# T masked before the weight split, no GpSimd copy, and hinted branches at the head of a LoRA feed-forward kernel

## The chip, the cores and the metric

The kernel runs on 1 core of one Trainium2 chip. The metric is device time in microseconds (us) of one execution. Three runs of the kernel before took 905.58, 907.25 and 908.7 us, the median is 907.25 us.

## The reference

Input `x` has 128 sequences of 32 tokens with 512 features, all float32; `itok_B_2_6` gives each sequence one of 16 LoRA adapters (values 2 to 6 are drawn). With B[i], A[i] chosen by a sequence's adapter:

```
lora_add(base, inp, A, B) = base + 0.5 * (inp @ A[i].T) @ B[i].T        # rank 16
gate = lora_add(x @ W_gate.T, x, A_gate, B_gate)                        # 512 -> 1376
up   = lora_add(x @ W_up.T,   x, A_up,   B_up)
act  = silu(gate) * up
down = lora_add(act @ W_down.T, act, A_down, B_down)                    # 1376 -> 512
amax = clip(max(|down|, axis=-1), 1e-5)
out  = x + (down / amax) @ levels[weight_2bit].T * (amax * weight_scale) + bias
```

## The kernel before

The host sorts nothing. The kernel itself ranks the 128 sequences by adapter (the "plan": `make_plan` on VectorE and one TensorE product, L1945), so that a tile of 512 tokens (16 sequences) holds at most two adapters. A flag `plan_flag` says whether this is so; each of the five engines reads it (`pair_flag`, L399) and branches to `wide_program` (8 tiles of 512 tokens, which is what runs on these inputs) or `general_program` (16 tiles of 256 tokens). On SyncE and TensorE the wide part is the `Else` of the branch (L730, L1954) and lies behind the whole general part in the program; on the other three engines it is the `If`.

Float32 products are made of three products of split numbers: ScalarE copies the high part of an operand (`_hi`), VectorE subtracts it from the whole for the low part (`_lo`), and TensorE multiplies high by high, low by high and high by low (`PASSES`). The 1376 inner features are 11 chunks, the first 96 wide and ten 128 wide. The 32 unused columns of the first chunk's weights hold the LoRA A matrices of the tile's two adapters, so that the first chunk's products (`first_tile_chunks` for tile 0, L1781) also give t = A x in 32 partitions of the banks `pw_gate` and `pw_up`. VectorE multiplies this t with a mask of 0.5 and 0 that keeps each token's own adapter (`wide_mask_t`, L1370). The masked t is written three times into `wt_split`: its high part in rows 0 to 31 (ScalarE, `wide_t_hi`, L1006), its low part in rows 32 to 63 (VectorE, `wide_t_lo`, L1375), and its high part again in rows 64 to 95 (semaphore `t_hi_again`). The B matrices are laid out to match in `wb_split` (ScalarE L999 for 64 rows, VectorE L1347 for 32), so that one product of 96 rows (`wide_lora`, L1813) adds the LoRA term. TensorE waits for `t_lo`, `t_hi_again` and `b_lo` before the first of these, and for `wgu_lo` (weights of chunk f split) and `silu_done` before the products of chunk f from 2 on (L1771).

The order of work is written out by hand for each engine. In tile 0 weights still come in: ScalarE and SyncE ask for gate and up weights (`load_wgu`, 512 KB each) and down weights (`load_wd`), two staging places each, and an ask for chunk f waits for the split of chunk f - 2. In tile 0 the second copy of the high part is made by GpSimd (L823); in the others by ScalarE. In tile 0, x comes in 16 entries of 64 KB (one sequence each, from a place that is read out of the plan, `load_x_entry`, L329): entries 0 to 7 (`x_raw`) by SyncE and ScalarE in turn before the branch, entries 8 to 15 (`x_more`) after it, three by ScalarE (`FROM_POOL` is 3) and five by GpSimd. SyncE's wide program begins with the mask, the two adapter numbers and the B rows (`load_wide_b`, L370).

TensorE runs 13 and 17 warm-up products ahead of its branch and 7 after it (`warm_up`, L1762), and then the products of tile 0, first for the first 256 tokens, then for the second.

Of the kernel before, what the change touches and what calls it, by code (L numbers as in the profile page):

```python
# [10 lines left out]
ALU = mybir.AluOpType  # L11
# [17 lines left out]
PAIR = 2 * RANK  # L29
# [14 lines left out]
WIDE = 512  # L44
# [24 lines left out]
FROM_POOL = 3  # L69
# [13 lines left out]
def build(nc, x_tok, x_feat, lora_index, places, pair_masks, w_gu, w_down, w_2bit, a_gu, a_down, b_rows,  # L83
          scale_col, bias_rows,
          block_mask_in, identity_in, out):
    with ExitStack() as ctx:
# [380 lines left out]
        def _(sp):  # L467
# [157 lines left out]
            def wide_program():  # L625
                load_mask(sp, 0, mask_gu, mask_gu_in)
# [97 lines left out]

            sp.dma_start(idx_places, lora_index).then_inc(index_in, 16)
# [4 lines left out]
            with sp.If(flag == 0):  # L730
                general_program()
            with sp.Else():
                wide_program()

        @block.gpsimd
        def _(pool):
# [81 lines left out]
            def wide_program():  # L818
                for e in range(FROM_POOL, ENTRIES):
                    load_x_entry(pool, wide_place(0, ENTRIES + e), x_more[:, e, :], pool_x_in)  # L820
                for g in range(2):
                    pool.wait_ge(t_masked, g + 1)
                    pool.tensor_tensor(wt_split[2 * PAIR:STACK, g, :], t_full[:, g, :],  # L823
                                       ones[0:PAIR, :].to_broadcast([PAIR, WIDE]), ALU.mult).then_inc(t_hi_again, 1)
                wide_split_bd(0, first=True)
                wide_split_a(1)
                pool.wait_ge(const_in, 48)
                with pool.Fori(1, WTILES - 1) as tile:
                    wide_split_a(tile + 1)
                    wide_split_bd(tile)  # L830
                    for s in range(WSUBS):
                        bias_residual(tile - 1, s)
                pool.wait_ge(residual_biased, WSUBS * (WTILES - 2))
                wide_split_bd(WTILES - 1)
                for s in range(WSUBS):
                    bias_residual(WTILES - 2, s)
                pool.wait_ge(late_res_in, 16 * WENTRIES)
                for s in range(WSUBS):
                    late = x_late[s // 2][:, s % 2, :]
                    pool.tensor_tensor(late, late, bias[:, :], ALU.add).then_inc(residual_biased, 1)  # L840
# [14 lines left out]
        def _(act):  # L855
# [146 lines left out]
            def wide_t_hi(tile, g, first):  # L1002
                act.wait_ge(t_masked, 2 * tile + g + 1)

                for first_row, done in (((0, t_hi),) if first else ((0, t_hi), (2 * PAIR, t_hi_again))):
                    nc.scalar.activation(wt_split[first_row:first_row + PAIR, g, :], t_full[:, g, :], ACT.Copy  # L1006
                                         ).then_inc(done, 1)
# [45 lines left out]
            def wide_tile(tile, first):  # L1053
# [7 lines left out]
                if first:  # L1061
                    for e in range(1, FROM_POOL):
                        load_x_entry(act, wide_place(0, ENTRIES + e), x_more[:, e, :], x_more_in)
                    load_wgu(act, 2)
                wide_x_hi(tile, 1, first)
                if first:
# [5 lines left out]
                    wide_t_hi(tile, 0, first)  # L1072
                    wide_t_hi(tile, 1, first)
                    split_hi_wd(0)
                else:
# [3 lines left out]
                    wide_t_hi(tile, 0, first)  # L1079
                    wide_t_hi(tile, 1, first)  # L1080
# [72 lines left out]
        def _(dve):  # L1153
# [277 lines left out]
            def wide_tile(tile, first):  # L1431
# [8 lines left out]
                if first:  # L1440
                    split_lo_wgu(2)
                    wide_b_lo(tile, 0)
                    wide_b_lo(tile, 1)
                    wide_mask_t(tile, 0, pw_gate, first)
                    wide_mask_t(tile, 1, pw_up, first)
                    wide_t_lo(tile, 0)
                    wide_t_lo(tile, 1)
                    split_lo_wd(0)
# [143 lines left out]
        def _(pe):  # L1592
# [350 lines left out]

            pe.wait_ge(plan_steps, PLAN_COLUMNS_STEP)
# [9 lines left out]
            with pe.If(flag == 0):  # L1954
                general_program()
            with pe.Else():
                wide_program()

# [63 lines left out]
```

## Time and profile before

| | us |
|---|---|
| median of three runs | 907.25 |
| lowest, highest | 905.58, 908.7 |
| profiled execution | 907.95 |
| its span | 906.1 |
| TensorE busy in it | 890.4 |
| VectorE, ScalarE, GpSimd busy | 350.9, 259.2, 87.2 |

The span runs from the first to the last instruction of one profiled execution, the time around it is 1.85 us. PE is TensorE, DVE VectorE, ACT ScalarE, POOL GpSimd, SP SyncE; a q behind a name is the sequencer of the engine, which reads registers, branches and issues DMAs. A time in the rows counts from the start of the span. "Idle before" is how long an engine did nothing ahead of a group, with what ended it.

### The profile page before, as it was taken

To read this page: it belongs to the slowest core of one execution; us is meant where nothing else is said; L and a number is where in the kernel's file an instruction comes from. 1 tells how busy PE (TensorE), PEld (TensorE's weight loads), DVE (VectorE), ACT (ScalarE), POOL (GpSimd) and SP (SyncE) were. 2 spreads that over 40 slices of the span, in tenths; PEclk is the share of its full clock that TensorE was granted. 3 is DMA by queue.
4 is the path that set the end of the run, shared out by engine and by line. 5 is a ranking of instruction groups with operands and counts; after the bars stand their busy time and mean duration, and the time that the engine had idled before them with its cause. 6 is when DMAs were issued, how large, how long until landed. Compare 5 with 4: busy or idle time off the path is not lost.

```text
span 906.1 us, 13800 instructions
## 1 busy us (share of the span) xinstructions
PE 890.4 (98%) x3991; PEld 720.2 (79%) x3991; DVE 350.9 (39%) x757; ACT 259.2 (29%) x448; POOL 87.2 (10%) x119
## 2 busy tenths in 40 slices
PE   6899999999999999999999999999999999999997
PEld 6788888888888887888888888788878888788885
DVE  4755264233442225422453224432245322552225
ACT  2533252122422124211242113421143111522112
POOL 1111003000030000310003100031001210100200
PEclk9999999999999999999999999999999999999999
DMA  5563110211112011120111102111111111201001
GB/s 144 166 192 109 39 56 22 51 30 33 47 35 59 21 45 45 31 62 12 50 48 38 47 12 57 52 38 35 27 45 52 43 33 30 56 24 34 24 14 47
DMA packets 44661, 45.38 MB, mean 50 GB/s; under 512 B 13168, under 2 KB 31088, under 8 KB 44608
## 3 DMA queue, kind: packets, MB, share of 16 engines
q1 hardware_dynamic: 42208, 41.52, 16.9%
q10 hardware_dynamic: 2176, 2.89, 1.1%
q0 software_dynamic: 224, 0.46, 0.2%
q14 instruction: 43, 0.35, 0.1%
q8 instruction: 10, 0.16, 0.1%
HBM read 36.44 MB, written 8.39 MB: 49 GB/s over the span
## 4 chain that ended last, share of the span: by engine, by line
PE 95%; DVE 1%; DMA 1%; ACT 0%; issue 0%; SPq 0%; ACTq 0%; DVEq 0%
PE pw_up L1771 26%; PE pw_gate L1771 24%; PE pw_down L1844 24%; PE ps_misc L1872 6%; PE pw_td L1833 5%; PE pw_down L1857 2%; PE pw_up L1813 2%; PE ps_misc L1771 2%; PE pw_gate L1813 2%; PE ps_misc L1864 1%; DMA rows<-w_gu 1%; DMA x_raw<-x_feat 0%; DVE wt_split L1375 0%; DMA plan_room<-places 0%; PE ps_misc L1813 0%
## 5 line engine op out<-in xcount | busy, mean ns | idle before, releaser
L1844 PE MATMUL pw_down<-wd,wact_split 128*128 128x512 f32 x960 | 232.5, 391 | 0.0
L1771 PE MATMUL pw_up<-wxs,wgu 128*128 128x512 f32 x948 | 229.4, 391 | 0.0
L1844 PEld LDWEIGHTS pw_down<-wd,wact_split 128*128 128x128 f32 x960 | 180.3, 188 | 44.5
L1771 PE MATMUL pw_gate<-wxs,wgu 128*128 128x512 f32 x864 | 212.8, 395 | 0.1
L1771 PEld LDWEIGHTS pw_up<-wxs,wgu 128*128 128x128 f32 x948 | 178.4, 188 | 38.6
L1771 PEld LDWEIGHTS pw_gate<-wxs,wgu 128*128 128x128 f32 x864 | 161.2, 189 | 33.6 <-issue 0.5
L1395 DVE TENSOR_TENSOR wact_full<-pw_up,wact_full 128x512 f32<-128x512 f32 (+1 forms) x87 | 60.0, 690 | 297.2 <-PE pw_up L1813 294.9
L1025 ACT ACTIVATE wact_full<-pw_gate 128x512 f32<-128x512 f32 (+1 forms) x80 | 47.7, 597 | 279.3 <-PE pw_gate L1813 279.3
L1037 ACT ACTIVATE wact_split<-wact_full 128x512 fp32r<-128x512 f32 x80 | 50.5, 631 | 69.7 <-DVE wact_full L1395 69.7
L1400 DVE TENSOR_TENSOR wact_split<-wact_full,wact_split 128x512 fp32r<-128x512 f32 x80 | 55.7, 697 | 26.3 <-ACT wact_split L1037 26.3
L815 POOL TENSOR_TENSOR rows<-rows,bias 128x512 f32<-128x512 f32 x28 | 35.8, 1288 | 222.3 <-DMA rows<-x_tok 221.1
L1872 PE MATMUL ps_misc<-wq,wdt_split 128*128 128x512 f32 x224 | 55.3, 389 | 0.0
L792 POOL TENSOR_TENSOR wgu_first<-wa_raw,scales 128x64 fp32r<-128x64 f32 x28 | 8.3, 327 | 446.8 <-DMA wa_raw<-a_gu 446.8
L1833 PE MATMUL pw_td<-wact_split,wad_split 128*32 128x512 f32 (+1 forms) x160 | 50.4, 397 | 0.0
L1872 PEld LDWEIGHTS ps_misc<-wq,wdt_split 128*128 128x128 f32 x224 | 42.0, 188 | 8.7
L1428 DVE SCALAR_TENSOR_TENSOR rows<-ps_misc,scales,rows 128x512 f32<-128x512 f32 x28 | 21.0, 751 | 71.8 <-PE ps_misc L1872 57.5
L999 ACT ACTIVATE wb_split<-low_room 64x256 fp32r<-64x256 f32 x40 | 16.8, 420 | 97.2 <-PE pw_up L1813 97.2
L1813 PE MATMUL pw_up<-wt_split,wb_split 96*128 96x512 f32 (+1 forms) x87 | 34.1, 392 | 0.0
L1813 PE MATMUL pw_gate<-wt_split,wb_split 96*128 96x512 f32 (+1 forms) x80 | 31.7, 396 | 2.3 <-DVE wt_split L1375 2.3
L1421 DVE TENSOR_TENSOR wdt_split<-ps_misc,wdt_split 128x512 fp32r<-128x512 f32 x28 | 19.3, 689 | 37.5 <-ACT wdt_split L1050 37.5
L999 ACT ACTIVATE wb_split<-wb_raw 64x256 fp32r<-64x256 f32 (+1 forms) x48 | 18.6, 403 | 47.8 <-PE pw_up L1813 47.2
L1006 ACT ACTIVATE wt_split<-wact_full 32x512 fp32r<-32x512 f32 x30 | 18.9, 630 | 41.0 <-DVE wact_full L1370 40.4
(137 smaller groups left out, 678.2 us busy)
## 6 DMA issues: line engine op xcount, KB each, us to landing
out<-rows SPq DMA_DIRECT2D x121, 64.0 KB, 1.6
rows<-x_tok SPq DMA_DIRECT2D x112, 64.0 KB, 1.8
rows<-w_gu SPq DMA_DIRECT2D x8, 512.0 KB, 3.9
x_raw<-x_feat SPq DMA_DIRECT2D x60, 64.0 KB, 1.7
x_more<-x_feat SPq DMA_DIRECT2D x56, 64.0 KB, 1.8
wb_raw<-b_rows SPq DMA_DIRECT2D x32, 92.0 KB, 2.9
low_room<-b_rows SPq DMA_DIRECT2D x32, 80.0 KB, 2.5
rows<-w_down SPq DMA_DIRECT2D x9, 256.0 KB, 4.1
```

The source lines that it names most:

```text
L815: pool.tensor_tensor(wx_res[:, s % 2, :], wx_res[:, s % 2, :], bias[:, :], ALU.add).then_inc(residual_biased, 1)
L999: nc.scalar.activation(wb_split[0:2 * PAIR, f % 2, :, 0:WIDTHS[f]], wb_raw_chunk(f), ACT.Copy).then_inc(b_hi, 1)
L1025: nc.scalar.activation(wact_full[0:w, f % 2, :], gate_bank(f)[0:w, :], ACT.Silu).then_inc(silu_done, 1)
L1037: nc.scalar.activation(wact(HI, f), wact_full[0:WIDTHS[f], f % 2, :], ACT.Copy).then_inc(act_hi, 1)
L1395: nc.vector.tensor_tensor(wact_full[0:w, f % 2, :], up_bank(f, first)[0:w, :], wact_full[0:w, f % 2, :], ALU.mult).then_inc(act_done, 1)
L1400: nc.vector.tensor_tensor(wact(LO, f), wact_full[0:WIDTHS[f], f % 2, :], wact(HI, f).bitcast(F32), ALU.subtract).then_inc(act_lo, 1)
L1428: nc.vector.scalar_tensor_tensor(wout[:, s, :], bank, ascale[:, s:s + 1], residual, ALU.mult, ALU.add).then_inc(out_ready, 1)
L1771: last = nc.tensor.matmul(bank, w, wxs[:, xp, k, :], start=(n == 0 and k == 0), stop=False, skip_group_check=(f == 0))
L1813: nc.tensor.matmul(bank[0:w, :], wb_split[0:STACK, f % 2, g, 0:w], wt_split[0:STACK, g, :], start=False, stop=True, skip_group_check=(f == ...
L1833: last = nc.tensor.matmul(pw_td[0:m, :], wad_split[0:w, f % 2, 0:m], wact(part, f), start=(f == 0 and part == HI), stop=(f == FC - 1 and p ...
L1844: last = nc.tensor.matmul(pw_down[:, s, :], wact(ap, f)[:, s * P:(s + 1) * P], wd[:, wp, f, :], start=(f == 1 and n == 0), stop=False)
L1872: last = nc.tensor.matmul(bank, dt[:, part, k, :], wq[:, k, :], start=(part == HI and k == 0), stop=(part == LO and k == KC - 1))
```

## The change

VectorE masks t ahead of the B splits and of the weight split of chunk 2. GpSimd no longer copies the high part in tile 0; ScalarE makes both copies of both halves, first copies first, in all tiles. `FROM_POOL` goes from 3 to 5: GpSimd asks for x entries 13 to 15, ScalarE for 8 and 9, SyncE for 10 to 12, as the first thing of its wide program. On SyncE and TensorE a branch-hint instruction stands at the head of the program, and the branch to the wide part is marked likely.

```diff
--- before.py
+++ after.py
@@ -66,7 +66,8 @@
 LAST_BY_ACT = [range(0), range(2, 4), range(1, 4), range(2, 4)]
 
 
-FROM_POOL = 3
+FROM_SP = 2
+FROM_POOL = 5
 PLAN_COLUMNS_STEP = 8
 WQ_FROM = FC - KC
 
@@ -623,6 +624,8 @@
                                  .rearrange("a t n -> (a t) n")).then_inc(done, 16)
 
             def wide_program():
+                for e in range(FROM_SP, FROM_POOL):
+                    load_x_entry(sp, wide_place(0, ENTRIES + e), x_more[:, e, :], x_more_in)
                 load_mask(sp, 0, mask_gu, mask_gu_in)
                 idx = wide_loras(0)
                 load_wide_b(sp, idx, 0)
@@ -722,15 +725,21 @@
                     store_wide_at(sp, last, s, entries, places[s])
                 sp.wait_ge(stored, 16 * WENTRIES * WTILES)
 
+
+            to_wide = sp.mark_branch_hint_location()
             sp.dma_start(idx_places, lora_index).then_inc(index_in, 16)
             sp.wait_ge(plan_listed, 1)
             for e in range(0, ENTRIES, 2):
                 load_x_entry(sp, wide_place(0, e), x_raw[:, e, :], x_in)
             flag = pair_flag(sp)
-            with sp.If(flag == 0):
+            sp.br_cond(flag == 1, on_true="sp_wide", on_false="sp_general").branch_hint(to_wide)
+            with nc.body("sp_general", valid_engines=[mybir.EngineType.SP]):
                 general_program()
-            with sp.Else():
+                sp.br("sp_end")
+            with nc.body("sp_wide", valid_engines=[mybir.EngineType.SP]):
                 wide_program()
+                sp.br("sp_end")
+            nc.switch_bb("sp_end")
 
         @block.gpsimd
         def _(pool):
@@ -818,10 +827,6 @@
             def wide_program():
                 for e in range(FROM_POOL, ENTRIES):
                     load_x_entry(pool, wide_place(0, ENTRIES + e), x_more[:, e, :], pool_x_in)
-                for g in range(2):
-                    pool.wait_ge(t_masked, g + 1)
-                    pool.tensor_tensor(wt_split[2 * PAIR:STACK, g, :], t_full[:, g, :],
-                                       ones[0:PAIR, :].to_broadcast([PAIR, WIDE]), ALU.mult).then_inc(t_hi_again, 1)
                 wide_split_bd(0, first=True)
                 wide_split_a(1)
                 pool.wait_ge(const_in, 48)
@@ -999,12 +1004,13 @@
                 nc.scalar.activation(wb_split[0:2 * PAIR, f % 2, :, 0:WIDTHS[f]], wb_raw_chunk(f), ACT.Copy
                                      ).then_inc(b_hi, 1)
 
-            def wide_t_hi(tile, g, first):
-                act.wait_ge(t_masked, 2 * tile + g + 1)
-
-                for first_row, done in (((0, t_hi),) if first else ((0, t_hi), (2 * PAIR, t_hi_again))):
-                    nc.scalar.activation(wt_split[first_row:first_row + PAIR, g, :], t_full[:, g, :], ACT.Copy
-                                         ).then_inc(done, 1)
+            def wide_t_hi(tile):
+                for first_row, done in ((0, t_hi), (2 * PAIR, t_hi_again)):
+                    for g in range(2):
+                        if done is t_hi:
+                            act.wait_ge(t_masked, 2 * tile + g + 1)
+                        nc.scalar.activation(wt_split[first_row:first_row + PAIR, g, :], t_full[:, g, :], ACT.Copy
+                                             ).then_inc(done, 1)
 
             def wide_td_copy(tile):
                 act.wait_ge(td_done, FC * (tile + 1))
@@ -1059,7 +1065,7 @@
                     load_x_entry(act, wide_place(0, ENTRIES), x_more[:, 0, :], x_more_in)
                 wide_x_hi(tile, 0, first)
                 if first:
-                    for e in range(1, FROM_POOL):
+                    for e in range(1, FROM_SP):
                         load_x_entry(act, wide_place(0, ENTRIES + e), x_more[:, e, :], x_more_in)
                     load_wgu(act, 2)
                 wide_x_hi(tile, 1, first)
@@ -1069,15 +1075,13 @@
                     load_wd(act, 1)
                     wide_b_hi(tile, 0, first)
                     wide_b_hi(tile, 1, first)
-                    wide_t_hi(tile, 0, first)
-                    wide_t_hi(tile, 1, first)
+                    wide_t_hi(tile)
                     split_hi_wd(0)
                 else:
                     wide_act_hi(tile - 1, FC - 1, False)
                     wide_b_hi(tile, 0, first)
                     wide_b_hi(tile, 1, first)
-                    wide_t_hi(tile, 0, first)
-                    wide_t_hi(tile, 1, first)
+                    wide_t_hi(tile)
                     wide_td_copy(tile - 1)
                     wide_td_hi(tile - 1)
                 for f in range(FC):
@@ -1438,13 +1442,13 @@
                 wide_x_lo(tile, 0)
                 wide_x_lo(tile, 1)
                 if first:
-                    split_lo_wgu(2)
+                    wide_mask_t(tile, 0, pw_gate, first)
+                    wide_mask_t(tile, 1, pw_up, first)
                     wide_b_lo(tile, 0)
                     wide_b_lo(tile, 1)
-                    wide_mask_t(tile, 0, pw_gate, first)
-                    wide_mask_t(tile, 1, pw_up, first)
                     wide_t_lo(tile, 0)
                     wide_t_lo(tile, 1)
+                    split_lo_wgu(2)
                     split_lo_wd(0)
                 else:
                     wide_act_lo(tile - 1, FC - 1)
@@ -1941,6 +1945,8 @@
                 wide_ffn(last, 2, last_bank[2], last_dt(2))
                 wide_ffn(last, 3, last_bank[3], last_dt(3))
 
+
+            to_wide = pe.mark_branch_hint_location()
             pe.wait_ge(plan_steps, PLAN_COLUMNS_STEP)
             nc.tensor.matmul(ps_plan, plan_columns, one_hot, start=True, stop=True).then_inc(plan_gathered, 1)
             pe.wait_ge(wgu_hi, 2)
@@ -1951,10 +1957,14 @@
                 nc.tensor.matmul(pw_td[:, :], wgu_chunk(HI, 1)[:, 0, 0, :], wgu_chunk(HI, 1)[:, 0:2, :, :],
                                  start=True, stop=True)
             flag = pair_flag(pe)
-            with pe.If(flag == 0):
+            pe.br_cond(flag == 1, on_true="pe_wide", on_false="pe_general").branch_hint(to_wide)
+            with nc.body("pe_general", valid_engines=[mybir.EngineType.PE]):
                 general_program()
-            with pe.Else():
+                pe.br("pe_end")
+            with nc.body("pe_wide", valid_engines=[mybir.EngineType.PE]):
                 wide_program()
+                pe.br("pe_end")
+            nc.switch_bb("pe_end")
 
 
 def kernel(x, itok_B_2_6, L0_cond_W_gate, L0_cond_W_up, L0_cond_W_down, L0_cond_A_gate, L0_cond_B_gate,
```

## Rows read from the trace of the kernel before

**Rows 1.** Part 1 of the page: busy us, share of span, instructions.

```profile
PE 890.4 (98%) x3991; PEld 720.2 (79%) x3991; DVE 350.9 (39%) x757; ACT 259.2 (29%) x448; POOL 87.2 (10%) x119
```

**Rows 2.** Timeline, TensorE, 0 to 50 us: start, duration, group, [idle before].

```profile
15.05 1.10 PE L1762 MATMUL ps_misc<-wgu 128*128 128x256 f32 x7 [0.39 <-issue]
15.98 0.64 PE L1781 MATMUL pw_gate<-wxs,wgu_first 128*128 128x256 f32 x4
...
26.06 1.60 PE L1781 MATMUL pw_down<-wxs,wgu 128*128 128x256 f32 x12
29.96 0.47 PE L1813 MATMUL pw_gate<-wt_split,wb_split 96*96 96x512 f32 x1 [2.29 <-DVE wt_split L1375]
...
31.21 4.51 PE L1771 MATMUL pw_gate<-wxs,wgu 128*128 128x512 f32 x12
...
42.47 2.88 PE L1771 MATMUL pw_gate<-wxs,wgu 128*128 128x512 f32 x12
```

**Rows 3.** Busy time by window: window, length, engines, granted clock, DMA share, GB/s.

```profile
31.20:35.72 4.52, 4.51 (x13) 3.62 (x14) 4.21 (x8) 4.05 (x8) 0.00 (x0) 0.64 0.80 191
```

**Rows 4.** Timeline, all engines, 24 to 30 us.

```profile
24.13 1.23 DVE L1156 TENSOR_TENSOR wgu<-rows,wgu 128x1024 fp32r<-128x1024 f32 x1 [1.87 <-ACT wgu L858]
24.14 0.64 PE L1781 MATMUL pw_up<-wxs,wgu_first 128*128 128x256 f32 x4
...
24.52 0.67 ACT L999 ACTIVATE wb_split<-wb_raw 64x192 fp32r<-64x192 f32 x2 [0.42 <-DMA wb_raw<-b_rows]
...
26.10 0.69 DVE L1370 TENSOR_TENSOR wact_full<-pw_gate,low_room 32x512 f32<-32x512 f32 x1
...
26.83 1.24 ACT L1006 ACTIVATE wt_split<-wact_full 32x512 fp32r<-32x512 f32 x2 [1.64 <-DVE wact_full L1370]
26.88 2.48 POOL L823 TENSOR_TENSOR wt_split<-wact_full,scales 32x512 fp32r<-32x512 f32 x2 [9.65 <-DVE wact_full L1370]
27.49 2.41 DVE L1375 TENSOR_TENSOR wt_split<-wact_full,wt_split 32x512 fp32r<-32x512 f32 x2
```

**Rows 5.** Line L1375 over the whole run: ns min/median/max, first and last start.

```profile
L1375 DVE TENSOR_TENSOR wt_split<-wact_full,wt_split x16: 681/683/1516, 27.5 to 782.0; 32x512 fp32r<-32x512 f32 x16
```

**Rows 6.** Lines L730, L381, L384 and L1954, columns as in rows 5.

```profile
L730 SPq COMPARE_BRANCH  x1: 50/50/50, 12.2 to 12.2; - x1
...
L381 SPq TENSOR_LOAD <-plan x16: 263/268/460, 14.7 to 879.5; - x16
...
L384 SPq MOVE low_room<-pair_masks x1: 29/29/29, 15.4 to 15.4; - x1
L384 SPq DMA_DIRECT2D low_room<-pair_masks x1: 354/354/354, 16.8 to 16.8; - x1
...
L1954 PEldq COMPARE_BRANCH  x1: 3659/3659/3659, 11.3 to 11.3; - x1
```

**Rows 7.** Timeline, SyncE's queue, 0 to 50 us.

```profile
7.91 3.70 SPq L329 DMA_DIRECT2D x_raw<-x_feat  x4
...
18.69 1.75 SPq L370 DMA_DIRECT2D wb_raw<-b_rows  x4
```

**Rows 8.** Chain; DMA issues of page and 0 to 40 us; queues 12 to 14 us; ScalarE.

```profile
11.27 3.42 DMA x_raw<-x_feat
...
x_raw<-x_feat SPq DMA_DIRECT2D x60, 64.0 KB, 1.7
...
x_more<-x_feat ACTq DMA_DIRECT2D x3, 64.0 KB, 2.9
...
q8 instruction: 1, 0.02, 3.4%
...
19.95 1.06 ACT L990 ACTIVATE wxs<-x_more 128x1024 fp32r<-128x1024 f32 x1 [4.17 <-DMA x_more<-x_feat]
```

**Rows 9.** Timeline, ScalarE, 37 to 47 us.

```profile
38.41 0.63 ACT L863 ACTIVATE wd<-rows 128x512 fp32r<-128x512 f32 x1 [2.54 <-DMA rows<-w_down]
...
39.90 0.58 ACT L1025 ACTIVATE wact_full<-pw_gate 128x512 f32<-128x512 f32 x1
```

## The prediction

> **What bounds the kernel now.** Read first the busy shares of the page: TensorE is busy 890.4 us of a span of 906.1 us [rows 1], so only what delays it can move the time, and nearly all its idle time is at the two ends. Then read TensorE in the timeline of the first 45 us [rows 2]. The reader is to see three places: 0.39 us idle ahead of the second warm-up, 2.29 us idle at 29.96 us ahead of the first tile's LoRA products, and twelve products from 31.21 us that take 4.51 us where the same twelve take 2.88 us at 42.47 us. The windows [rows 3] explain the third: in 31.20 to 35.72 us the mean granted clock is 0.64, a mix of full speed (2.4 GHz) and half (1.2 GHz), right behind the 2.29 us in which TensorE did nothing. So one hole costs twice: 2.29 us, and 4.51 - 2.88 = 1.6 us of slow products. The other engines in front of the hole [rows 4] show what made it. The two LoRA-A results are complete at 24.14 + 0.64 = 24.78 us, but VectorE masks them only from 26.10 us, after the weight split (1.23 us) and the two B splits. Then GpSimd copies (2.48 us for two) while VectorE subtracts, and VectorE's two subtractions take 2.41 us; over the whole run one takes 0.68 us in the median and 1.52 us at most [rows 5].
>
> **The change part by part.**
>
> *Mask first.* The mask products need their bank (first one about 24.3 us, second 24.78 us) and the mask, which SyncE asked for at 16.8 us. VectorE is idle then, so two masks of about 0.69 us end at 25.05 and about 25.7 us, against 27.4 us now. The mask is no longer what ScalarE waits for: it is the B rows. ScalarE starts on them at 24.52 us, waiting for their landing [rows 4], and its two B splits take 0.67 us, so it is free at 25.2 us.
>
> *No GpSimd copy, two more ScalarE copies.* ScalarE now makes four copies in a row. Two take 1.24 us, so four take 2.5 us: 25.2 to 27.7 us. VectorE's subtractions follow the second copy (26.4 us) and take 0.68 us each without GpSimd beside them: done at 27.15 us. So the fourth copy ends last, at 27.7 us, and it takes the place of the subtraction that ended at 29.90 us. TensorE's preceding products end at 26.06 + 1.60 = 27.66 us [rows 2], so it starts the LoRA products at about 27.75 us: the hole shrinks from 2.29 us to 0.1 us, 2.2 us gained. Removed from GpSimd are 2.48 us which nobody else waits for.
>
> *Weight split 2 moved behind.* It runs 27.15 to 28.4 us on VectorE. ScalarE's first down-weight split and first silu (0.63 and 0.58 us for one of each in [rows 9]) end at about 28.8 us, so the products of chunk 2 start at 28.85 us against 31.21 us: 2.35 us gained in all at this point. The split is not free (1.23 us) but lies beside the silu.
>
> *Clock.* With 0.1 us idle, then four LoRA products, then some 0.2 us idle, I take no fall of the granted clock: 1.6 us gained. From the other side it is 0, if the rest of the hole is enough for a fall; I take 1.6 because the only fall in these rows follows 2.29 us without any product.
>
> *What is late next.* TensorE's chunk 3 starts at 42.47 us [rows 2]; it needs silu 2, which ends at 39.90 + 0.58 = 40.48 us, held by a down-weight landing at 38.4 us [rows 9]. That is a cover of 2.0 us. This supply chain hangs on VectorE's order (down-weight split, ask, land), and VectorE comes to its first down-weight split at 28.4 us instead of 29.90 us (27.49 + 2.41): 1.5 to 1.6 us earlier. TensorE moves 2.35 + 1.6 = 3.95 us. 2.0 + 1.6 - 3.95 = -0.35 us: a wait of about 0.35 us appears there. For later chunks I take none.
>
> *SyncE's three x entries.* Each is a load of a register, a few register steps and a DMA: four take SyncE 3.70 us from the first DMA's start to the last one's end, and a DMA some 0.35 us [rows 6, 7], so it is 1.1 us from one to the next. Three put 3.3 us ahead of the mask and the B rows. One is taken from ScalarE, two from GpSimd, which did them without a stop. They are hidden as long as the split of the second half of x starts by about 20.6 us; it starts at 19.95 us now [rows 8], takes 1.06 us, and TensorE begins the second half midway between 15.98 us and the end of the last group's issue, 27.5 us, at 21.7 us.
>
> *SyncE's hint.* SyncE's branch is recorded at 12.2 us with 0.05 us, and its next instruction starts at 14.7 us [rows 6]: 2.4 us in which nothing is issued. Five instructions later it stands again: the register step at 15.4 us, the DMA it belongs to at 16.8 us, 1.3 us, where a whole x entry takes 1.1 us. If the hint removes the first stop, the second still can stand, since the code behind the target is asked for only after the jump. With the first stop gone alone, x is asked for at 14.4, 15.5 and 16.6 us, the mask at 17.7 us (16.8 now), and the B rows from 19.6 us (18.69 now), last landing up to 25.4 us. With both gone all is 1.4 us earlier: B rows from 18.2 us, landing about 23.6 us. I take 24.5 us, as now: the B rows lie between these, and ScalarE's weight chunk 2 is asked for 1.1 us earlier and leaves the engines room. The ends are -0.9 and +0.9 us for the LoRA start, the earlier one capped by TensorE at 27.66 us.
>
> The Trainium skill (Runtime: NRT & Kernel Launch, "Instruction fetch mechanics") says that prefetch is purely sequential, over two lines, and that a taken branch out of the window forces a fetch. The trace agrees on the fetch, with the 2.4 us above. On whether a hint helps, the rule speaks against the change: by it the sum would be that of the second rival below.
>
> *TensorE's hint.* Its branch takes 3.66 us, from 11.3 us [rows 6], but it stands beside queued warm-up products, and only 0.39 us of idle comes through. Behind it the first real product needs the split of x: landed at 11.27 + 3.42 = 14.69 us, split 1.06 us, 15.75 us; it starts at 15.98 us. So I count 0, with 0.15 us gain as one end; the cover is the x transfer. The other end is below zero: both code transfers move to the head of the program, where the two loads that the plan waits for are under way. One code transfer filled 3.4% of 16 engines in 2 us [rows 8], that is 1.1 us of one engine, so up to 1.1 us late for everything.
>
> **The sum.** The profiled execution took 907.95 us (span 906.1 us and 1.85 us around it). 907.95 - 2.35 - 1.6 + 0.35 = 904.35 us. The median of the three runs shown is 907.25 us, 0.7 us under the profiled one, and their spread (905.58 to 908.7) is wide enough that a clock fall may be missing in one. I take half of the 0.7 us off: 904.0 us. A measurement tells 0.3%, 2.7 us, from no change; the forecast is 3.25 us under the median, so it is just above it.
>
> **Rivals.**
>
> 1. *The plan is late.* The two early code transfers delay the plan's loads. For it: 1.1 us of one engine. Against: two loads at the same time use 16 engines and only a part meets it. Everything shifts 1.1 us: 904.35 + 1.1 = 905.45 us, or 905.1 us with the same 0.35 us off, 0.2% faster, no change by the measurement.
>
> 2. *The other side: SyncE's stop stays.* The hint doesn't bring the code, and x, mask and B rows are queued behind the jump. Then x is asked for at 16.8, 17.9 and 19.0 us; with the 2.9 us that ScalarE's three take now in the median [rows 8] it lands at 21.9 us, is split at 23.0 us, and TensorE's second half starts 1.25 us late and ends at 28.9 us. The B rows go from 22.0 to 23.4 us and land at 27.8 us with the present 4.4 us (last asked for at 18.69 + 1.75 - 0.37 = 20.07 us, used at 24.52 us). From the landing to chunk 2 it is 0.7 + 2.5 + 1.15 = 4.4 us: 32.2 us, against 31.21 us, with a hole of 2.2 us and the clock fall again. 907.95 + 1.0 = 908.95 us. It decides from a landing of the B rows at 26.8 us on, or 28.4 us if the clock stays. For it: GpSimd and ScalarE would have asked for these entries without any jump far away. Against: it needs the hint to do nothing.
>
> 3. *More than forecast.* The last x entry takes 3.42 us where the median of SyncE's is 1.7 us, and a code transfer runs in 12 to 14 us [rows 8]. If TensorE's hint moves it away, x lands at 11.27 + 1.7 = 13.0 us and TensorE starts when its warm-up ends, about 15.5 us: 0.5 us earlier; ScalarE's later requests too, so that the wait of 0.35 us goes: 904.0 - 0.85 = 903.15 us. Against: the code behind the target may be fetched at the same moment.
>
> **How the numbers follow.** Forecast 0.58 (its own range 903.0 to 905.3, two thirds of it more than 0.3% under the median), rival 1 0.20, rival 2 0.10, rival 3 0.12. The range 902.7 to 906.8 us reaches to rivals 1 and 3 and leaves rival 2 out. Faster: 0.39 + 0.12 = 0.51. Slower by over 0.3% needs 909.97 us, half of rival 2 at most, and some of nothing foreseen: 0.06. Within: 0.43.
>
> **What would show it.** After the change: the LoRA products at 27.7 to 28 us; the row of clock over the next twelve products at 1.00 and these in 2.9 us; VectorE's two subtractions 1.4 us; ScalarE's four copies in a row ending last; SyncE's first x entry at or before 14.5 us; chunk 3 with a small wait for silu 2. A LoRA start after 29 us released by ScalarE's copies would show that the B rows are late; a start of the first real product after 16.5 us would show rival 1. The steady tiles should not move. I am wrong if TensorE gets a new wait there or SyncE's entries come after 16.8 us.

## The result

The changed kernel takes 908.73 us in the median of 20 runs (907.57 to 910.05). The kernel before, timed beside it in 20 runs, takes 905.62 us (904.73 to 909.73). The ratio is 1.0031, 95% interval 1.0023 to 1.0039: the change makes the kernel 3.1 us slower. Forecast were 904.0 us and at most 906.8 us: too low, and with the wrong sign. The profiled execution of the changed kernel took 908.18 us with a span of 906.4 us, the one of before 907.95 us.

The kernel before has runs of two kinds. Every run comes with its mean granted clock. Of 114 runs of the kernel before that were made beside the experiments, 61 have a clock of 0.999 or more and a median of 905.36 us, and 53 have 0.998 or less and 907.95 us. The execution from which everything was read was one of the latter (0.997). Of the changed kernel's 20 runs 16 have 0.998 or less. The fall of the clock in [rows 3], 0.36 of full speed over 4.52 us, is 0.0018 of a mean over 906 us, so a run at 0.999 or more has room for little of it (an estimate: none of those runs was profiled). The clock compares only runs of one kernel, since it also counts the time behind TensorE's last product. And since the median of the kernel before moves with the share of each kind, the ratio is the firmer of the two figures given for a run.

The profiled pair shows little of the 3.1 us: the two executions are 0.23 us apart. Of the 3.1 us, 2.3 are what the profiled execution of before lies over its own median, and 0.55 what the changed kernel's lies under its own.

The busy time of TensorE is what it was [rows 1]:

```profile
PE 890.9 (98%) x3991; PEld 720.7 (80%) x3991; DVE 349.6 (39%) x757; ACT 259.7 (29%) x450; POOL 84.6 (9%) x115
```

TensorE in the timeline of the first 50 us, against [rows 2]:

```profile
6.90 0.74 PE L1951 MATMUL ps_misc<-plan_room 128*96 128x128 f32 x2 [6.90 <-DVE plan_room L1562]
...
17.75 0.88 PE L1785 MATMUL pw_gate<-wxs,wgu_first 128*128 128x256 f32 x4 [1.80 <-ACT wxs L995]
25.07 0.64 PE L1785 MATMUL pw_gate<-wxs,wgu_first 128*128 128x256 f32 x4
31.06 0.48 PE L1817 MATMUL pw_gate<-wt_split,wb_split 96*96 96x512 f32 x1
32.32 3.01 PE L1775 MATMUL pw_gate<-wxs,wgu 128*128 128x512 f32 x12
39.26 0.62 PE L1837 MATMUL pw_td<-wact_split,wad_split 128*32 128x512 f32 x2 [0.26 <-DVE wact_split L1404]
42.76 2.99 PE L1775 MATMUL pw_gate<-wxs,wgu 128*128 128x512 f32 x12 [0.16 <-ACT wact_full L1031]
```

Three things are to be seen. The hole in front of the LoRA products is closed (31.06 us, no idle), and the twelve products behind it take 3.01 us instead of 4.51 us. But the first real product comes at 17.75 us instead of 15.98 us, behind 1.80 us without work, and from it to the second half (the same group of products for the second 256 tokens) at 25.07 us it is 7.32 us. What was gained at 30 us was lost before 25 us, and chunk 3 begins at 42.76 us against 42.47 us. From there to the end of the span both take 863.6 us: the steady tiles didn't move.

The windows (length, the engines, granted clock, DMA share, GB/s) show where the clock fell:

```profile
17.75:21.72 3.97, 3.97 (x20) 3.97 (x21) 1.11 (x1) 0.00 (x0) 0.00 (x0) 0.57 0.77 212
21.72:30.90 9.18, 9.18 (x78) 9.07 (x76) 4.39 (x7) 5.13 (x9) 0.00 (x0) 1.00 0.64 163
31.00:35.00 4.00, 3.85 (x16) 2.86 (x17) 3.62 (x8) 2.44 (x6) 0.00 (x0) 1.00 0.21 56
```

TensorE idles 1.80 us, and behind that the mean granted clock is 0.57 for 4 us, near the lower of its two levels (1.2 GHz); the fall that stood at 31.20 us [rows 3] stands at 17.75 us instead.

Why the start is late: the DMA queues and issues (last number: us to landing) of 1 to 4 us, then the same load and the plan's product in the kernel before.

```profile
q8 instruction: 1, 0.02, 2.0%
plan_room<-lora_index SPq DMA_DIRECT2D x1, 64.5 KB, 3.5
```

```profile
plan_room<-lora_index SPq DMA_DIRECT2D x1, 64.5 KB, 2.0
5.62 0.74 PE L1945 MATMUL ps_misc<-plan_room 128*96 128x128 f32 x2 [5.62 <-DVE plan_room L1558]
```

A transfer of instructions, 16 KB, now runs beside the two loads that the plan waits for, and the adapter numbers land after 3.5 us, not 2.0 us as before. The plan's product starts at 6.90 us; before it was 5.62 us. Everything that is read from a place in the plan is asked for 1.3 us later. The chain of waits gives the rest of the way to the first real product:

```profile
11.50 3.95 DMA first_a<-a_gu
15.48 0.26 ACT wgu_first L1063
```

The first tile's A matrices, which ScalarE scales ahead of its split of x, land at 15.45 us; before they were scaled from 12.48 us and x was the last to come. 1.3 us from the plan and 0.5 us from this landing make the 1.8 us. The landing takes 4.0 us here, and 3.6 to 4.1 us in the three other kernels with the hint at TensorE's head, against 2.4 to 2.9 us in all kernels without it there. Another transfer of instructions, from 13.4 us, runs beside it; that this transfer is the cause was not tried apart.

SyncE's queue, in its timeline, against [rows 7]; the source rows of the two branches, and the register loads behind SyncE's, against [rows 6]:

```profile
16.75 2.54 SPq L330 DMA_DIRECT2D x_more<-x_feat  x3
...
21.91 1.76 SPq L371 DMA_DIRECT2D wb_raw<-b_rows  x4
```

```profile
L735 SPq COMPARE_BRANCH  x1: 75/75/75, 13.5 to 13.5; - x1
L1960 PEldq COMPARE_BRANCH  x1: 383/383/383, 11.6 to 11.6; - x1
L318 SPq TENSOR_LOAD <-plan x3: 273/275/287, 16.0 to 18.2; - x3
```

TensorE's hint does what its name says: the branch takes 0.38 us instead of 3.66 us. SyncE's does not: from the end of its branch at 13.6 us to the next instruction at 16.0 us it is still 2.4 us. So the B rows are asked for from 21.91 us, and ScalarE starts on them 2.9 us later than before, as its and VectorE's timeline shows (against [rows 4]):

```profile
27.42 0.67 ACT L1004 ACTIVATE wb_split<-wb_raw 64x192 fp32r<-64x192 f32 x2 [2.66 <-DMA wb_raw<-b_rows]
27.67 0.69 DVE L1374 TENSOR_TENSOR wact_full<-pw_gate,low_room 32x512 f32<-32x512 f32 x1 [2.60 <-PE pw_gate L1785]
28.40 2.42 ACT L1012 ACTIVATE wt_split<-wact_full 32x512 fp32r<-32x512 f32 x4 [0.31 <-DVE wact_full L1374]
29.72 1.28 DVE L1379 TENSOR_TENSOR wt_split<-wact_full,wt_split 32x512 fp32r<-32x512 f32 x2
```

The T part itself (masks first, four ScalarE copies, no GpSimd copy) is as forecast: four copies in 2.42 us, two subtractions in 1.28 us instead of 2.41 us [rows 4]. The late B rows cost nothing here only because TensorE is late too.

### The profile page after: what moved, and what is told of

Its sections match the earlier page's. It is cut to its first block, busy times and chain, and to the rows that moved or that the text cites. A ratio compares the mean times of both kernels' runs of the same rounds, so it can differ in the third digit from the quotient of the medians.

```text
span 906.4 us, 13802 instructions
## 1 busy us (share of the span) xinstructions
PE 890.9 (98%) x3991; PEld 720.7 (80%) x3991; DVE 349.6 (39%) x757; ACT 259.7 (29%) x450; POOL 84.6 (9%) x115
## 4 chain that ended last, share of the span: by engine, by line
PE 95%; DVE 2%; DMA 1%; ACT 1%; issue 0%; POOLq 0%; ACTq 0%; POOL 0%; DVEq 0%; SPq 0%
PE pw_up L1775 26%; PE pw_down L1848 24%; PE pw_gate L1775 24%; PE ps_misc L1876 6%; PE pw_td L1837 4%; PE pw_down L1861 2%; PE pw_up L1817 2%; PE ps_misc L1775 2%; PE pw_gate L1817 2%; PE ps_misc L1868 1%; DMA rows<-w_down 0%; DMA first_a<-a_gu 0%; PE pw_gate L1785 0%; DMA plan_room<-lora_index 0%; PE pw_up L1785 0%
```

## The experiments

Line numbers shift by a few between kernels. "Over before" is a difference of medians to the kernel before on the same chip; the ratio is that of the runs, with its 95% interval. Where that interval holds 1.000, no change is shown, whatever the medians say. The edits are shown shortened, with "..." for what is left out.

### First question: which of the two hints costs?

**Without both hints.** The changed kernel less its hint instructions.

```diff
-            to_wide = sp.mark_branch_hint_location()
-            sp.br_cond(...).branch_hint(to_wide)
+            sp.br_cond(...)
```

The same goes on TensorE.

> The changed kernel without its two hints; all else stays. Theory A (the code transfer that TensorE's hint starts at 2.06 us, beside the plan's loads, is the loss): the adapter list lands at 2.9 us again instead of 4.48 us, the plan's first step starts at 3.2 instead of 4.5 us, the first real product at 16 us instead of 17.75 us, and the time is 2.5 us or more under the changed kernel: 905 to 906 us. Theory B (the loss is the three x entries behind SyncE's jump): the first product starts earlier but the second half waits for x, the B rows stay late, and the time stays within 0.8 us of the changed kernel (908.7).

909.18 us, 2.7 over before, ratio 1.0028 (1.0015 to 1.0041). Taking the hints away did not bring the gain back. TensorE's and ScalarE's timelines:

```profile
28.07 0.67 ACT L1003 ACTIVATE wb_split<-wb_raw 64x192 fp32r<-64x192 f32 x2 [4.67 <-DMA wb_raw<-b_rows]
31.04 0.45 PE L1816 MATMUL pw_gate<-wt_split,wb_split 96*96 96x512 f32 x1 [2.54 <-ACT wt_split L1011]
32.37 4.20 PE L1774 MATMUL pw_gate<-wxs,wgu 128*128 128x512 f32 x12
```

The start is in time again (16.18 us, and the second half at 22.49 us), but the B rows are late, the LoRA products wait 2.54 us and the clock falls behind them: the second rival of the prediction, hole and all.

**SyncE's hint alone.**

```diff
-            to_wide = pe.mark_branch_hint_location()
...
-            pe.br_cond(flag == 1, on_true="pe_wide", on_false="pe_general").branch_hint(to_wide)
+            pe.br_cond(flag == 1, on_true="pe_wide", on_false="pe_general")
```

> The changed kernel with SyncE's hint alone. Both theories: SyncE's hint does nothing, its branch stands 2.4 us, no code transfer of 8 KB between 0 and 13 us, and the time is that of the kernel without hints, within 0.5 us. If SyncE's hint costs something of its own, it is over 0.5 us slower than that.

907.99 us, 1.5 over before, ratio 1.0012 (1.0001 to 1.0023). SyncE's register steps and DMAs of the x entries, this kernel first, then the one without hints:

```profile
L330 SPq MOVE x_more<-x_feat x3: 29/29/29, 15.6 to 18.1; - x3
L330 SPq DMA_DIRECT2D x_more<-x_feat x3: 333/346/644, 15.6 to 18.2; - x3
```

```profile
L330 SPq MOVE x_more<-x_feat x3: 29/29/38, 15.6 to 19.6; - x3
L330 SPq DMA_DIRECT2D x_more<-x_feat x3: 333/333/347, 17.4 to 19.7; - x3
```

The first stop, behind the branch, is the same. The second, 1.8 us between a register step and its DMA, is gone, and no transfer of instructions came before the branch. So either the hint acts on the second stop, or the two instructions that it adds shift the wide part in the program.

**TensorE's hint alone.** The changed kernel less SyncE's hint.

> The changed kernel with TensorE's hint alone. Theory A: as slow as the changed kernel (908.2 to 909.2), with the transfer of 16 KB at 2 us and the plan 1.3 us late. Theory B expects the same as without hints, since TensorE's branch is hidden behind queued warm-up products.

910.7 us, 4.2 over before, ratio 1.0042 (1.0027 to 1.0056): the dearest of the four, and 1.5 us above the range that either theory had room for. The plan's product comes at 7.55 us, the LoRA products at 34.31 us behind 4.19 us idle: late plan and late B rows add up here.

**TensorE's hint in the kernel before.** To carry the hint, TensorE's `If` and `Else` are also written as `br_cond` with two bodies, as in the changed kernel.

> The kernel before with TensorE's hint and nothing else of the change. Theory A: 1.3 to 3.5 us slower than before (907 to 909), plan 1.3 us late, first product at 17.3 us or later. Theory B: no change, within 0.3 us of before.

908.66 us, 2.2 over before, ratio 1.0027 (1.0015 to 1.004).

```profile
18.32 1.12 PE L1781 MATMUL pw_gate<-wxs,wgu_first 128*128 128x256 f32 x4 [2.09 <-ACT wxs L990]
```

With the hint, and so far not parted from the other form of the branch, it costs 2.2 us: the plan's product comes at 7.44 us, TensorE stands 2.09 us, and the next products run at about half speed (1.05 us for four that otherwise take 0.64 us).

### Second question: what is the T part worth, and can SyncE's stop be moved away?

**T part alone:** mask first, four ScalarE copies, no GpSimd copy; branches and x entries as before.

```diff
-FROM_SP = 2
-FROM_POOL = 5
+FROM_SP = 3
+FROM_POOL = 3
```
The hints are out too. SyncE and TensorE keep `br_cond` in place of `If`; what that does by itself was not measured, but SyncE asks for mask and B rows at 16.92 and 18.82 us, as before within 0.2 us.

> The part on T alone: masks first, no GpSimd copy, two more ScalarE copies; the x entries as before (ScalarE 3, GpSimd 5), no hints. Theory M (this part closes the hole, the rest of the change opened others): LoRA products at 27.7 to 28.1 us with under 0.5 us idle ahead, no fall of the clock behind them, 1.5 to 3.5 us under before. Theory C (ScalarE's two more copies are the new bound and eat the gain): LoRA products after 29 us released by ScalarE's last copy, within 0.5 us of before.

904.82 us (904.24 to 906.02), 1.45 under before, ratio 0.9981 (0.997 to 0.9993). All 12 runs have a clock of 0.999 or more.

```profile
16.09 0.64 PE L1784 MATMUL pw_gate<-wxs,wgu_first 128*128 128x256 f32 x4
...
21.84 0.64 PE L1784 MATMUL pw_gate<-wxs,wgu_first 128*128 128x256 f32 x4
...
23.44 0.67 ACT L1003 ACTIVATE wb_split<-wb_raw 64x192 fp32r<-64x192 f32 x2 [0.71 <-DMA wb_raw<-b_rows]
25.17 2.42 ACT L1011 ACTIVATE wt_split<-wact_full 32x512 fp32r<-32x512 f32 x4 [1.06 <-DVE wact_full L1373]
27.83 0.47 PE L1816 MATMUL pw_gate<-wt_split,wb_split 96*96 96x512 f32 x1
29.09 3.04 PE L1774 MATMUL pw_gate<-wxs,wgu 128*128 128x512 f32 x12
```

Forecast were 27.75 us and 28.85 us for the LoRA products and for the twelve of chunk 2. ScalarE's four copies start on time for another reason than forecast: the B rows came early, and what it waited for was the mask.

**Arms exchanged:** the changed kernel without hints, the wide part as the first arm of the branch on SyncE and TensorE.

```diff
-            sp.br_cond(flag == 1, on_true="sp_wide", on_false="sp_general").branch_hint(to_wide)
-            with nc.body("sp_general", valid_engines=[mybir.EngineType.SP]):
+            with sp.If(flag == 1):
+                wide_program()
+            with sp.Else():
                 general_program()
...
```

> The changed kernel without hints and with the arms of the branch exchanged on SyncE and TensorE, so that the wide part lies directly behind the branch; SyncE's three x entries stay. Theory J (what made the entries and the B rows late is the far jump): SyncE asks for x at 13.0, 14.1 and 15.2 us and for B rows from 18.3 us, TensorE's branch takes under 0.5 us, LoRA products at 27.8 us or earlier, 2 to 4 us under before. Theory O (the order itself, three entries ahead of the B rows, costs): B rows used after 25.5 us and no gain over before.

908.78 us, 2.5 over before, ratio 1.0022 (1.0011 to 1.0032). The head is as hoped, and TensorE is ahead of the T part's kernel:

```profile
27.67 0.44 PE L1812 MATMUL pw_gate<-wt_split,wb_split 96*96 96x512 f32 x1 [0.20 <-DVE wt_split L1374]
```

But the branches have only moved. At the end of the wide arm each of the two engines now jumps over the general part. SyncE's source rows, its wait for the last stores and ScalarE's requests for stores, first of this kernel, then of the T part alone:

```profile
L734 SPq COMPARE_BRANCH  x2: 38/42/45, 12.3 to 904.1; - x2
L87 SPq DRAIN  x1: 57/57/57, 906.6 to 906.6; - x1
SPq L734 <- DMA out<-rows: 3.9, 1, 3.9
L397 ACTq DMA_DIRECT2D out<-rows x7: 322/387/1959, 896.6 to 902.4; - x7
```

```profile
L740 SPq COMPARE_BRANCH  x1: 38/38/38, 902.3 to 902.3; - x1
L87 SPq DRAIN  x1: 13/13/13, 902.5 to 902.5; - x1
SPq L740 <- DMA out<-rows: 2.1, 1, 2.1
L397 ACTq DMA_DIRECT2D out<-rows x7: 322/352/387, 896.7 to 900.1; - x7
```

From the last branch to SyncE's drain at the end it is 2.5 us instead of 0.2 us, and the last store takes SyncE 3.9 us of waiting instead of 2.1 us. The second goes with TensorE's own jump: between 895 and 901 us two transfers of instructions of 16 KB run on TensorE's queue, and one of ScalarE's requests takes 1.96 us. The T part alone and the next kernel, where only SyncE's arms are exchanged, have neither transfer there, and SyncE waits 2.1 and 2.4 us.

**T part with SyncE's arms exchanged.** The same edit on SyncE alone, on top of the T part.

> The part on T alone with the arms exchanged on SyncE only; x entries as before. If the jump matters only for what is queued behind it, mask and B rows are asked for 3.9 us earlier, LoRA products at 27.7 us (TensorE's own end), and the time is that of the part on T alone or up to 1 us under it.

907.2 us, 0.9 over before and 2.4 over the T part alone, ratio 1.0007 (0.9996 to 1.0017).

```profile
L87 SPq DRAIN  x1: 58/58/58, 904.8 to 904.8; - x1
```

The drain stands 2.5 us behind SyncE's last branch at 902.3 us: the far jump costs the same at either end, and at the end nothing hides it. The mean clock of this execution is 0.997, though every window up to 900 us has 1.00: the longer end alone lowers it.

**Padding instead of the hint:** the kernel without hints, with nine instructions added in SyncE's general part, which is never run.

```diff
             def general_program():
+                for e in range(3):
+                    entry_at(sp, narrow_place(0, e))
                 idx = tile_loras(0)
```

> The changed kernel without hints and with nine instructions more in SyncE's general part, which is never run: they only move the wide part in the program. Theory P (SyncE's hint helped by where it placed the target against the 128-instruction transfers, not by fetching it): the first stop of 2.5 us stays, the second stop of 1.8 us (at 15.6 us) is gone as with SyncE's hint, x is asked for at 15.6, 16.7 and 17.8 us, and the time is that of the kernel with SyncE's hint alone, 1.2 us under the kernel without hints. Theory H (the hint itself does it): both stops stay and the time is that without hints, 909.2 us.

907.05 us, 0.8 over before, ratio 0.9998 (0.9985 to 1.0012): no change to before, and 1.9 us less over before than without the nine instructions.

```profile
L330 SPq MOVE x_more<-x_feat x3: 29/29/29, 15.7 to 18.1; - x3
L330 SPq DMA_DIRECT2D x_more<-x_feat x3: 333/346/540, 15.7 to 18.1; - x3
```

The second stop is gone without any hint. So no fetch by the hint is needed for that; where the wide part lies in the program is enough. The windows show one thing more. Both kernels stand 2.0 us ahead of the LoRA products (1.99 us with the hint, at 30.65 us; 2.00 us with the padding, at 30.57 us), and the clock behind it fell in the first alone:

```profile
30.00:34.00 4.00, 3.27 (x10) 2.35 (x11) 3.62 (x8) 2.90 (x7) 0.00 (x0) 0.77 0.21 71
```

```profile
30.00:34.00 4.00, 3.35 (x14) 2.48 (x15) 3.62 (x8) 2.91 (x6) 0.00 (x0) 1.00 0.24 68
```

### Third question: the parts one by one

**x entries alone,** in the kernel before.

```diff
-FROM_POOL = 3
+FROM_SP = 2
+FROM_POOL = 5
```
with SyncE's loop over three entries.

> The kernel before with the x entries dealt out as in the change (SyncE 3, GpSimd 3, ScalarE 2) and nothing else: no hints, T masked late, GpSimd's copy kept. If the entries behind SyncE's jump are the loss, x is split for the second half after 21.4 us and B rows after 27 us, and since here the mask stands behind the B splits, the LoRA products start at 32.5 to 33.5 us: 3 to 4.5 us over before. If the entries are covered, no change within 0.5 us.

911.77 us, 5.6 over before, ratio 1.0049 (1.0032 to 1.0066), 1.1 us more than the most that was expected.

```profile
33.45 0.74 PE L1816 MATMUL pw_gate<-wt_split,wb_split 96*96 96x512 f32 x1 [5.32 <-DVE wt_split L1378]
28.45 0.67 ACT L1002 ACTIVATE wb_split<-wb_raw 64x192 fp32r<-64x192 f32 x2 [5.44 <-DMA wb_raw<-b_rows]
```

With the old order on VectorE the mask waits behind the B splits, and a late B row holds everything: the x entries cost 5.6 us here, and 4.2 us with the T part (from 1.45 under to 2.7 over before).

**T part, TensorE's hint behind the plan's product.**

```diff
-            to_wide = pe.mark_branch_hint_location()
...
             nc.tensor.matmul(ps_plan, ...)
+            to_wide = pe.mark_branch_hint_location()
```

> The part on T with TensorE's hint placed behind the plan's product (5.6 us) instead of at the head. If the hint's harm is only that its transfer meets the plan's loads, the transfer of 16 KB is at about 7 us, the plan is on time (product at 5.6 us), TensorE's branch takes under 0.5 us, and the time is that of the part on T alone within 0.6 us. If a hinted jump costs in itself (the block behind the target asked for at another moment), it is over 0.8 us slower than the part on T alone.

904.76 us, 1.4 under before, ratio 0.9979 (0.9964 to 0.9993): no different from the T part alone. The transfer runs at 6.63 us, the plan's product at 5.52 us.

**T part, TensorE's hint at the head.**

> The part on T with TensorE's hint at the head as in the change, x entries as before. Transfer at 2 us meets the plan's loads: one of the two lands 1.3 to 2 us late, plan product at 6.9 to 7.5 us, first real product 1.5 to 2.3 us later than without the hint, and 2 to 3.5 us over the part on T alone.

907.39 us, 1.2 over before, ratio 0.9998 (0.9983 to 1.0012); beside its twin with the late hint, on the same chip, 2.6 us more. Only the place of the hint differs. The plan's product comes at 7.78 us. The load of the ranking's other input and TensorE's first real product, first with the hint at the head, then the load with the late hint:

```profile
plan_room<-places ACTq DMA_DIRECT2D x1, 64.5 KB, 4.5
18.81 1.16 PE L1784 MATMUL pw_gate<-wxs,wgu_first 128*128 128x256 f32 x4 [2.19 <-ACT wxs L994]
```

```profile
plan_room<-places ACTq DMA_DIRECT2D x1, 64.5 KB, 2.2
```

The code transfer delays one of the two loads, not always the same one: the adapter numbers in the changed kernel, `places` in the three others with this hint (4.2 to 4.5 us), where the plan's product is 1.8 to 2.3 us late instead of 1.3 us.

**T part with the padding on SyncE.**

> The part on T with SyncE's wide part moved by nine instructions that are never run, x entries as before, no hints. SyncE's second stop goes (1.3 us), mask and B rows are asked for 1.3 us earlier. TensorE's own end (27.7 us) is what the LoRA products wait for already, so I expect no change from the part on T alone within 0.4 us; if the B rows still bound, 0.5 to 1.3 us faster.

904.67 us, 1.5 under before, ratio 0.9978 (0.9963 to 0.9992). The B rows are asked for at 17.2 us, but then nothing waits for them.

### Last question: would the hints work in another place?

**SyncE's hint just ahead of its branch,** behind the x entries, in the changed kernel without TensorE's hint.

```diff
             for e in range(0, ENTRIES, 2):
                 load_x_entry(sp, wide_place(0, e), x_raw[:, e, :], x_in)
+            to_wide = sp.mark_branch_hint_location()
             flag = pair_flag(sp)
```

> The changed kernel without TensorE's hint and with SyncE's hint placed behind its four x entries, about 0.6 us ahead of the jump, instead of at the head. If the hint works when the target is asked for shortly before, a transfer of 8 KB starts at 12 to 12.6 us and the stop at the jump shrinks from 2.6 us to under 2 us. If SyncE's hint brings nothing wherever it stands, the stop stays 2.5 to 2.7 us, and since the target is placed as with the hint at the head, the second stop stays away and the time is that of SyncE's hint alone, 1.5 us over before, within 0.6 us.

908.26 us, 2.5 over before, ratio 1.0017 (1.0004 to 1.003). In 12 to 22 us:

```profile
L318 SPq TENSOR_LOAD <-plan x3: 269/272/288, 14.9 to 17.6; - x3
```

The branch is at 12.18 us, the next instruction at 14.9 us: the stop is there in full. SyncE's hint fetched nothing early in either place. The 1.5 us over before that were expected within 0.6 us were missed by 1.0 us; the time itself is 0.3 us from that of SyncE's hint at the head, and the rest is the lower median of the kernel before on this chip (905.75 against 906.45 us).

**The changed kernel with TensorE's hint behind the plan's product.**

> The changed kernel with TensorE's hint moved behind the plan's product, all else as changed (SyncE's hint at the head, three x entries). If the meeting with the plan's loads is TensorE's hint's whole cost, the plan's product starts at 5.6 us instead of 6.9 us and the time is that of SyncE's hint alone, 1.5 us over before within 0.5 us, against 2.8 us over before for the changed kernel. If the hint costs in another way too, it stays over 2.3 us over before.

906.79 us, 1.0 over before, ratio 1.0004 (0.9992 to 1.0016), against 3.1 over for the changed kernel. The hint's place alone gives back 2.1 us (by differences to before, on two chips), and what is left is SyncE's: the LoRA products come at 30.06 us behind 2.07 us idle.

## Why the prediction was wrong

Two steps failed, and each was there as a rival. Either is enough to take the gain away: the T part with TensorE's hint at the head is 1.2 us over before (no change by its ratio), with the x entries 2.7 us over.

- **"TensorE's hint": "So I count 0".** The other end that the step names, code transfers that meet the plan's loads, is what happened, and its size was too small: "up to 1.1 us late for everything" left out that a late start has a price of its own. The first real product came 1.8 us late, and the 1.80 us of idle ahead of it was followed by a fall of the clock: from there to the second half 7.32 us instead of 5.75 us (21.84 less 16.09 us in the T part alone), 1.6 us more. Measured at the head it costs 2.2 us (kernel before) and 2.6 us (T part), and 1.5 us on top of the x entries (4.2 against 2.7 over before); behind the plan's product nothing (904.76 against 904.82 us). Rival 1 had the mechanism with a chance of 0.20 and priced it at 1.1 us.
- **"SyncE's hint": "With the first stop gone alone".** The first stop never went, with the hint at the head or at the branch. The second, which I left standing, did go, and padding does the same. With the stop in place the three x entries push the B rows to where rival 2 put them: it said they land at 27.8 us, in the kernel without hints ScalarE takes them at 28.07 us, with a hole of 2.54 us (forecast 2.2) and the fall. Its price was 4.6 us over the forecast's sum (908.95 less 904.35), measured are 4.2 us. The working of that rival was right, and 0.10 was too low a chance for it. The Trainium skill (Runtime: NRT & Kernel Launch, "Instruction fetch mechanics") says that a taken branch out of the prefetched window has to fetch its target before anything goes on. The traces agree: SyncE stops for 2.4 to 2.7 us at its far jump, at the head or, with its arms exchanged, at the end.

The parts add up roughly: T part -1.45, x entries +4.2, the second stop gone -1.9 (2.7 to 0.8 over before, with the padding; with SyncE's hint itself it was -1.2), TensorE's hint +2.6, together 3.45 us, against 3.1 us measured. The hint's +2.6 was taken without the x entries, and the two delays lie partly beside each other: the B rows are late while TensorE is late anyway.

- **"Clock": 1.6 us gained.** A mis-sized term. It was read from one execution of the kind that 53 of 114 runs are. The prediction saw that "a clock fall may be missing in one" of its three runs, and took 0.35 us off for it. Against those 53 runs (907.95 us) the T part gains 3.1 us, close to the 3.6 us of the sum; against the other 61 (905.36 us) 0.5 us. Without any clock term the steps still gave 2.0 us. Why only 0.5 us of it is seen against the 61 stays open, as none of them was profiled. The two kinds are 2.6 us apart where the fall is priced at 1.6 us, so something else than the fall, a shorter hole perhaps, must be worth some 1.0 us in them.
- **Right:** mask first and the four copies (27.83 us for 27.75), chunk 2 (29.09 us for 28.85), the subtractions (1.28 us for 1.4), the closed hole and full clock behind it (3.01 us), the steady tiles. The Trainium skill (SBUF — State Buffer, "SBUF: two separate sides") says that VectorE and GpSimd share a pair of ports, and that a VectorE operation with two SBUF inputs and a GpSimd operation that reads SBUF hold it exclusively, one fully blocking the other. The trace agrees in direction: without the GpSimd copy beside them two subtractions take 1.28 us instead of 2.41 us; the lock itself was not tried apart.
- **Right in part, by luck:** the copies started at 25.17 us for the 25.2 us forecast, but they waited for the mask and not for the B rows, which the T part had 1.1 us before the 24.5 us taken. Of the 0.35 us of wait for silu 2 ahead of chunk 3 the changed kernel has 0.16 us and the T part none; 0.26 and 0.23 us stand elsewhere, ahead of products of `pw_td`.
- **Rival 3** did not come either: x was no longer what TensorE's start waited for, the A matrices were, which landed at 15.45 us. In the T part with the late hint the start came at 15.64 us instead of 16.09 us, but the second half then waited 0.96 us for x, and the time stayed.

Nothing beat the T part alone. With padding or a late TensorE hint it is the same within the intervals, 904.67 to 904.82 us, 0.2% under the kernel before.

## What to carry to other kernels

A prefetch moves a transfer, it doesn't remove it: ask what it meets where it goes, and put it behind the load that everything waits for. Before requests are queued behind a far jump, price them as if the hint did nothing, and change owner only if that price can be paid. And look at the spread of the runs before you count a clock fall that one profile shows: here over half of the runs of the kernel before left room for next to none, by their mean clock, and of the 3.6 us forecast 1.45 us were measured.

## What the runs showed of the hardware

- A hint at the head shortens TensorE's branch from 3.66 to 0.38 us. Its 16 KB transfer starts about 2 us into the span, and one of two loads of 64.5 KB beside it takes 3.5 to 4.5 us instead of 1.9 to 2.4 us. On SyncE no transfer of 8 KB is seen ahead of the branch, with a hint or without.
- A far jump on SyncE costs 2.4 to 2.7 us in each place that was measured, at the head and as the last thing of the program.
- Nine instructions that never run can take a stop of 1.8 us away, by where they put the code behind them: 909.18 against 907.05 us (2.7 and 0.8 over before).
- Behind 1.99 us of idle the granted clock fell (0.77 in the window of 30 to 34 us), and behind 2.00 us at the same place of a kernel that does the same it stayed at 1.00. So the length of the idle time alone does not settle it. That this is also what makes the two kinds of runs of the kernel before, 2.6 us apart, is likely but not shown.
